# Two identity products ahead of the second and the fourth step of the second attention

## The reference

```python
x = x + _L0_xcond_ref(_layernorm(x), ctx_1024, ctx_1024, condB_tau[:, None], fside_BxS2_0, ...)
x = x + _L0_ffn_ref(_layernorm(x), ...)      # 64 experts, 8 chosen, and a shared one
x = x + _L1_xcond_ref(_layernorm(x), ctx_1024, ctx_1024, condB_tau[:, None], fside_BxS2_0, ...)
x = x + _L1_ffn_ref(_layernorm(x), ...)      # 8 experts, 2 chosen
```

```python
scores = jnp.einsum('blhe,bshe->bhls', qh, kh)
scores = scores * tau[:, None, None, :] + delta[:, None, None, :]
a = jax.nn.softmax(scale * scores, axis=-1)
out = jnp.einsum('bhls,bshd->blhd', a, vh).reshape(B, L, D)
return out @ Wo.T + bo
```

## Time and profile before

| | |
|---|---|
| median of 3 runs | 1312.14 us (1311.17 to 1317.81) |
| span of the profiled execution | 1393.2 us |
| TensorE busy, whole span | 1262.3 us, 91% |
| VectorE / ScalarE / GpSimd busy | 830.6 / 492.7 / 559.0 us |
| mean granted clock, whole span | 0.938 |

### The profile page before, as it was taken

The page is one execution under the profiler, slowest core; times in us unless marked ns, Lnnn a source line. Parts: engine busy times, 40 slices in busy tenths (PEclk is TensorE's granted clock), DMA queues, the critical chain, the costliest instruction groups (busy, mean ns, idle before and its releaser), DMA issues. The chain is left out here.

```text
span 1393.2 us, 40465 instructions
## 1 busy us (share of the span) xinstructions
PE 1262.3 (91%) x12894; PEld 973.0 (70%) x12895; DVE 830.6 (60%) x2642; ACT 492.7 (35%) x1255; POOL 559.0 (40%) x706
## 2 busy tenths in 40 slices
PE   6999999999768999998669999999999889999995
PEld 3666666666536988887336666656666679999995
DVE  3467777777566666665445676666666454444442
ACT  2554454544402433433124444444444212121211
POOL 2226565564551011001554565665642313333332
PEclk9999999999968999999758997888899989999998
DMA  4335444465516778854222333223221513433423
GB/s 113 113 106 153 132 133 145 126 190 157 170 60 197 199 210 251 241 158 133 63 62 78 89 86 84 76 84 85 76 69 42 199 34 79 118 102 102 140 48 79
DMA packets 115804, 166.65 MB, mean 120 GB/s; under 512 B 26480, under 2 KB 96768, under 8 KB 114672
## 3 DMA queue, kind: packets, MB, share of 16 engines
q0 software_dynamic: 22672, 58.41, 15.8%
q1 hardware_dynamic: 46496, 54.35, 13.5%
q10 hardware_dynamic: 46560, 52.98, 12.0%
HBM read 87.82 MB, written 63.49 MB: 109 GB/s over the span
## 5 line engine op out<-in xcount | busy, mean ns | idle before, releaser
L1047 DVE TENSOR_REDUCE mx<-banks 112x2 f32<-112x750 f32 x256 | 235.6, 935 | 122.4 <-PE banks L627 109.9
L1894 POOL DMA_INDIRECT xs_d<-xns,idx x160 | 155.2, 970 | 177.2 <-PE banks L653 131.2
L1567 ACT ACTIVATE shared_buf<-banks 125x672 f32<-125x672 f32 x256 | 172.9, 727 | 89.3 <-PE banks L653 78.9
L1908 POOL DMA_INDIRECT kept<-y_d,yidx x128 | 125.2, 978 | 139.3 <-issue 86.7
L919 PEld LDWEIGHTS banks<-xT,attn_buf 128*128 128x128 f32 x1364 | 159.7, 195 | 5.1 <-DVE xT L1433 3.6
L919 PE MATMUL banks<-xT,attn_buf 128*128 128x128 f32 x1364 | 160.1, 278 | 3.3 <-DVE xT L1433 3.3
L653 PE MATMUL banks<-attn_buf 18*125 18x112 f32 x3072 | 129.7, 292 | 33.1 <-DVE mx L1047 21.6
L864 PE MATMUL banks<-xT,staged 128*128 128x128 f32 x1064 | 142.8, 277 | 7.0 <-DVE staged L1444 6.5
L653 PEld LDWEIGHTS banks<-attn_buf 18*125 18x125 f32 x3072 | 104.3, 190 | 63.3 <-issue 34.5
L864 PEld LDWEIGHTS banks<-xT,staged 128*128 128x128 f32 x1064 | 129.1, 192 | 12.1 <-DVE xT L1433 8.1
L627 PE MATMUL banks<-attn_buf 17*112 17x375 f32 x1024 | 121.8, 547 | 9.2 <-ACT shared_buf L1567 8.8
(11 more groups left out here) (214 smaller groups left out, 1954.3 us busy)
## 6 DMA issues: line engine op xcount, KB each, us to landing
shared_buf<-xs_d SPq DMA_DIRECT2D x136, 128.0 KB, 2.5
y_d<-shared_buf ACTq DMA_DIRECT2D x132, 128.0 KB, 2.6
ringbuf<-in_we SPq DMA_DIRECT2D x6, 2176.0 KB, 8.3
ringbuf<-in_we POOLq DMA_DIRECT2D x32, 384.0 KB, 4.6
attn_buf<-attn_buf SPq DMA_DIRECT2D x128, 93.8 KB
attn_buf<-in_ctxT ACTq DMA_DIRECT2D x29, 375.0 KB
xs_d<-zrow ACTq DMA_DIRECT2D x16, 512.0 KB
y_d<-zrow ACTq DMA_DIRECT2D x16, 512.0 KB
```

What stands on the lines that cost most here:

```text
L1047: dve.tensor_reduce(mx[:, i % 2, 2 * p:2 * p + 2], banks[0:Q, 2 * p:2 * p + 2, 0:S], AX.X, ALU.max).then_inc(s_max, 1)
L1567: act.activation(pT[:, slot:slot + 2, :], banks[0:KT, first_bank:first_bank + 2, 0:ST * Q], ACT.Exp, scale=0.25).then_inc(s_exp, 1)
L1894: pool.indirect_dma_start(xs_d[L.number], bass.IndirectOffsetOnAxis(ap=idx[:, b % 2, k:k + 1], axis=0), rows, None).then_inc(s_scat[b % 2] ...
L1908: pool.indirect_dma_start(yg[:, u, k, :], None, y_d, bass.IndirectOffsetOnAxis(ap=yidx[:, u, k:k + 1], axis=0)).then_inc(s_gat[u][k * 4 // ...
```

## The change

Two `idle` products were issued ahead of `scores_T` of step 2 (`i == 1`) in the first attention only. Now they are issued at that place in both attentions, and in the second attention also ahead of `scores_T` of step 4 (`i == 3`). The first batch of each attention goes by a table of its own and stays as it was.

```diff
@@ -640,7 +640,7 @@ scores_T
                     wait(pe, s_exp, g * 2)
                     if isinstance(b, int) and b == 0:
                         idle(FILL_SCORES[l][i], bank[SCORES_T[0]])
-                    elif l == 0 and i == 1:
+                    elif i == 1 or (l and i == 3):
                         idle(2, bank[SCORES_T[0]])
                     pe.wait_ge(s_mx[i % 2], n * (16 * NQ // 2) + 16 * (i // 2 + 1))
                     if i < 2 or in_layer(b, 1):
```

## The result

The changed kernel takes 1325.0 us (median of 17 runs, 1319.6 to 1332.9) against 1317.7 us of the kernel before (17 runs, 1309.4 to 1324.2). The ratio of the runs is 1.0074, with a 95% interval of 1.0053 to 1.0095: between 7.0 and 12.5 us slower (the medians alone differ by 7.3 us, which lies inside). The forecast was 11 us more, and 1323 us.

The account below looks back on a forecast made before the run. TensorE's order and clock bound the second attention. 30 pairs x 0.41 = 12.3 us, less 1.0 hidden, plus 1.2 at halved clock, is 12.5; with fewer falls 11, so 1312.1 + 11 = 1323 us, range 1300 to 1332.

Parts of the forecast that it names:

- The likeliest case: Second attention: pairs' cost paid, clock falls about as before or few in either; 1323 us, range 1317 to 1330, chance 0.48.
- The price of a pair is 0.41 us: From `O2T` to `scores_T`, 0.80 us with the pair against 0.39 without, read from the two attentions at full clock.
- Does it wait there? ... I take off 0.4 and 0.6: Waits at steps 2 and 4 hiding pairs: 0.4 us off for the last batch, 0.6 for the others; step 4 none.
- Is the delay taken up later?: Waits at step 3 or 1 start from TensorE and move with it; step 2 to 3 stays 6.27 us.
- Ordinary runs may have much fewer falls: Profiled span 81 us above the runs' median, 86 us clock lost; with fewer halved-clock stretches, 11 us cost is left.
- The fill holds the clock: Rival: pairs avert clock falls in the second attention; 1304 us with eight averted, 1294 with all and echoes; chance 0.27.
- Hidden: Rival: each pair shortens the next wait at step 3 or 1, time stays 1312 to 1316 us; chance 0.13.
- More falls: Rival: pairs shift timing in the second attention; three more clock falls at 2.5 us each, 1331 us; chance 0.12.

Follow-up runs that it names:

- The earlier normalisation: Kernel before (clamped counts), GpSimd's normalisation moved ahead of the fourth gather behind step 2, second attention; against kernel before 1.0059 late, 0.995 on time.

## Why the prediction was right or wrong

**The sign and the mechanism held.** The likeliest case was that the pairs' cost is paid and the clock's falls stay as they are. The cost was shown on time (full price of 0.86 us in each of batches 12 and 13, clock 1.00 with and without) and late (0.88 of the clock in both, 0.8 us more a batch). That the number came so near is partly luck. The forecast was 11 us on a base of 1312.1 us, the median of three runs; seventeen runs put that base at 1317.7, 5.6 us higher, and the added time came out some 1 to 4 us lower.

**"The price of a pair is 0.41 us"** held: 0.43 for the two places' mean in batches 12 and 13.

**"Does it wait there? ... I take off 0.4 and 0.6"** was the mis-sized term, together with **"Is the delay taken up later?"**, which I answered with no. About 1.0 us was to be hidden; in batches 2 to 11 alone it was 3.9. Per batch, against 0.43 for each pair: 0.16 from step 1 to step 2, mostly the wait ahead of step 2; 0.14 from step 3 to step 4, the wait ahead of `XT2`; 0.13 from step 4 to step 1, the wait for VectorE's maxima. I had argued from the first attention that waits move along with TensorE. Those at step 3 do. The one ahead of step 1 does only in part; without the pairs its size swings between 0.2 and 0.7 us from batch to batch. Why it swings was not followed up. The wait ahead of `XT2` was not in my profile at all. The cost of the two pairs is 10 x 0.43 in batches 2 to 11, 2 x 0.86 in 12 and 13 and 0.6 in batch 1, 6.7 us by the profiles' positions (start of batch 1 to start of batch 14: 292.4 us against 285.7). At the full price the pairs of batches 14 and 15 add at most 1.7 us to that, 8.4 in all, within the 7.0 to 12.5 us measured. The two profiles themselves lie 11.6 us apart: batch 0, which the change leaves alone, is 2.9 us longer in that of the changed kernel, and batches 14 and 15 are 4.2 us longer instead of at most 1.7. Why stays open.

**"Ordinary runs may have much fewer falls"** was right for the runs of the result, and my reason, 81 us of difference against 86 us of lost clock, pointed the right way. But that the two numbers agree is luck: the kernel before loses 34 us of full clock on time as well (a mean of 0.974 over 1314.3 us), so that the clock makes 52 us of the difference and the rest is not the clock's. In the first attention, at 1.00 in both, batches 6 to 13 take 174.3 us late and 170.1 on time. And I took the difference to be one of the profiled execution. It belonged to the whole series: all its runs take about 1396 us in two of them and 1318 in two others.

**"The fill holds the clock"**, the rival at 0.27, was wrong for steps 2 and 4 as they stand. Its idea was right elsewhere: late, fill at steps 1 and 3 cut ten falls to two, and the first attention loses its full clock without its pair at step 2. I had argued that this pair can't be what holds the clock, since it stands away from the waits, and the runs without it refuted that argument. Why a pair at step 2 holds the clock in the first attention and not in the second stays open. So does whether it holds it by TensorE's being busy or by when everything behind it comes. The earlier normalisation adds no product and took the clock from 0.88 to 0.83, so that timing alone can move it; no run put a pair's delay there without its products.

The Trainium skill, page "TensorE: Matmul & The Clock Gate", section "Why this matters for your kernels", advises to keep TensorE busy and to leave no long idle gaps between bursts of products. The first half agrees with the fill at steps 1 and 3, and not with that at steps 2 and 4. The second half is not enough here: in the profile of before the longest wait of TensorE in batches 2 to 11 is 1.26 us, and in the first attention without its pair the clock fell 0.9 us after a wait of 0.85.

**"Hidden"**, at 0.13, was half true of batches 2 to 11 and not of the rest. **"More falls"**, at 0.12, was not seen: late, twelve falls for ten, with the same 61 us at half the clock. The prediction priced falls by their number, 2.5 us each, but they last from 3 to 14 us, and what counts is the time at half the clock.

## What to carry to other kernels

Fill that is to keep TensorE's clock up is best tried first where the engine waits: 30 pairs of products cost nothing there where the clock held and won 0.6% where it fell; one job away from the waits they cost 0.7 to 0.9%. That they cost nothing in a wait was shown; what they do for the clock has to be measured, since the pairs at steps 2 and 4 won 1.9% once the normalisation came earlier. Before costing a stall from a profile, compare its span with the runs' times; where they are 6% apart the profile may show waits that the runs don't have, and both what it shows and what it covers up have to be doubted. Of a delay in front of waits for two other engines half was absorbed here (0.43 of 0.86 us a batch), so count the waits behind it in all stretches and not in the cleanest one.

## What was not expected of the hardware

The same kernel takes about 1318 us in two series and about 1396 us in two others, 6% more, reproducibly within a series (23 runs from 1388 to 1412 us in one, 35 from 1312 to 1327 in another). Each series ran on a chip of its own and no chip was used twice, so that it stays open whether the chip makes the difference or something else about the series. The slower kind is the one called late. In the late profiles 116 to 145 of TensorE's some 1400 raises of a semaphore come more than 0.5 us after the product's end, in the attentions up to 4.6 us, where the profiles on time have at most 10, none by more than 0.62. TensorE pauses within groups of small products, and the mean clock of the kernel before is 0.92 to 0.95 instead of 0.96 to 0.98. Of the 79 us between its late profile and its profile on time 7 lie in the first attention, 19 between the attentions, 52 in the second and 2 behind. What makes the semaphores late was not found, and nothing here tried to. An edit worth -0.5% in one kind of series was worth +0.6% in the other.
